# New orders for TensorE, ScalarE, VectorE and the one DMA queue in a convolution and attention kernel

## The reference

```python
# layer 0: 32 models of 16 channels; perception = x and its 8 shifts by one pixel, 144 channels a model
hdn = relu(einsum('bmchw,mdc->bmdhw', per_g, w1) + b1)          # 64 hidden channels a model
x = x + einsum('bmdhw,mcd->bmchw', hdn, w2) + b2
# layer 1: attention over the 1024 pixels, 128 inner channels
theta = einsum('oc,bcn->bno', theta_w, xf) + theta_b
phi = einsum('oc,bcn->bon', phi_w, xf) + phi_b[:, None]
g = einsum('oc,bcn->bno', g_w, xf) + g_b
attn = softmax(einsum('bno,bom->bnm', theta, phi), axis=-1)
z = einsum('co,bno->bcn', w_w, einsum('bnm,bmo->bno', attn, g)) + w_b
z = (z - bn_mean) * bn_gamma / sqrt(bn_var + 1e-5) + bn_beta
out = z + x
```

## Time and profile before

| | |
|---|---|
| median of 3 runs | 1632.85 us (1629.54 to 1635.52) |
| the profiled execution | 1621.29 us, of it the span of the profile 1619.5 us |
| TensorE matmuls | busy 1521.1 us, 94% of the span |
| VectorE, ScalarE, GpSimd | busy 867.7, 764.3 and 266.2 us |
| transfers | 361.84 MB, mean 223 GB/s |

### The profile page before, as it was taken

How to read it: one execution, slowest core, us unless ns; L and a number is a source line. 1 busy time by engine, 2 the same in 40 slices (tenths; PEclk the granted TensorE clock), 3 DMA queues, 4 the chain that set the end, 5 groups by cost and what they waited for, 6 DMA issues and landing times.

```text
span 1619.5 us, 23832 instructions
## 1 busy us (share of the span) xinstructions
PE 1521.1 (94%) x8324; PEld 846.5 (52%) x8324; DVE 867.7 (54%) x1200; ACT 764.3 (47%) x1205; POOL 266.2 (16%) x134
## 2 busy tenths in 40 slices
PE   5889989999998999999999999999999999999976
PEld 1265544655545455554655546455554655546455
DVE  0256363654636556383664646456383654637465
ACT  2444454544544455454544544455455544545542
POOL 0021030211203021030211203021030301204021
PEclk9999999999999999999999999999999999999998
DMA  9674875859667495875849658595875849677234
GB/s 290 163 266 160 253 261 159 295 168 284 231 187 257 165 322 191 256 255 160 295 160 288 236 170 284 170 308 190 259 258 164 296 157 294 220 214 271 96 119 167
DMA packets 179006, 361.84 MB, mean 223 GB/s; under 512 B 12336, under 2 KB 120880, under 8 KB 178992
## 3 DMA queue, kind: packets, MB, share of 16 engines
q1 hardware_dynamic: 178992, 361.66, 68.6%
HBM read 252.56 MB, written 109.05 MB: 223 GB/s over the span
## 4 chain that ended last, share of the span: by engine, by line
PE 78%; DMA 12%; DVE 4%; ACT 2%; issue 2%; SPq 1%; DVEq 0%; ACTq 0%
PE ps L413 24%; PE ps L433 8%; PE ps L424 7%; DMA x_lo<-rows_out 5%; PE ps L449 5%; PE ps L451 5%; PE ps L450 5%; DMA rows_out<-probs 4%; PE ps L479 4%; PE ps L481 4%; PE ps L480 4%; PE ps L493 2%; PE ps L464 2%; DVE probs L778 2%; PE ps L465 2%
## 5 line engine op out<-in xcount | busy, mean ns | idle before, releaser
L413 PE MATMUL ps<-windows,w_main 128*64 128x512 f32 x2048 | 488.2, 606 | 26.4 <-DMA windows<-in_x 13.2
L926 POOL TENSOR_TENSOR probs<-probs,row_inv 128x1024 f32<-128x1024 f32 x128 | 265.5, 2084 | 1326.2 <-DVE row_inv L766 1326.2
L611 ACT ACTIVATE hidden<-ps,columns 128x512 f32<-128x512 f32 x512 | 314.9, 688 | 309.5 <-PE ps L424 176.4
L413 PEld LDWEIGHTS ps<-windows,w_main 128*64 128x64 f32 x2048 | 129.4, 136 | 318.0 <-issue 203.0
L634 ACT ACTIVATE probs<-ps,neg_max 128x1024 f32<-128x1024 f32 x128 | 142.7, 1115 | 186.6 <-DVE neg_max L760 164.2
L741 DVE SCALAR_TENSOR_TENSOR x<-ps,columns,windows 128x512 f32<-128x512 f32 x128 | 95.9, 749 | 226.0 <-PE ps L433 195.5
L760 DVE TENSOR_REDUCE neg_max<-ps 128x1 f32<-128x1024 f32 x128 | 154.6, 1208 | 58.3 <-PE ps L466 56.1
L433 PE MATMUL ps<-hidden,w2s 128*32 128x512 f32 x1024 | 143.6, 634 | 32.3 <-ACT hidden L611 32.3
L787 DVE TENSOR_TENSOR x_lo<-x_lo,x_hi 128x1024 fp32r<-128x1024 f32 x128 | 165.2, 1301 | 15.3 <-ACT x_hi L641 15.2
L479 PE MATMUL ps<-x_hi,arena 128*128 128x256 f32 x512 | 152.6, 298 | 21.9 <-DVE arena L793 12.7
L778 DVE STREAM_TRANSPOSE probs<-probs 128x1024 f32<-128x1024 f32 x128 | 156.3, 1231 | 18.4 <-POOL probs L926 10.1
(11 more groups left out here) (55 smaller groups left out, 1520.8 us busy)
## 6 DMA issues: line engine op xcount, KB each, us to landing
windows<-in_x SPq DMA_DIRECT2D x208, 562.0 KB, 12.8
rows_out<-probs SPq DMA_DIRECT2D x128, 512.0 KB, 3.9
x_lo<-rows_out SPq DMA_DIRECT2D x128, 512.0 KB, 4.2
out<-x SPq DMA_DIRECT2D x64, 512.0 KB, 3.4
windows<-in_x SPq DMA_DIRECT2D x32, 421.5 KB, 9.6
windows<-in_x SPq DMA_DIRECT2D x32, 409.9 KB, 11.0
windows<-in_x SPq DMA_DIRECT2D x32, 281.0 KB, 7.1
rows_out<-hidden SPq DMA_DIRECT2D x16, 512.0 KB, 5.1
```

Source lines behind the costliest of these rows:

```text
L413: mm(ps[rows, hidden_bank(s, q), :], w_main[:, p, which, :], shifted(windows[:, w, :], unit // UNITS, half), start=True, stop=False, skip_ ...
L611: activation(hidden[:, q, :], ps[:, hidden_bank(s, q), :], ACT.Relu, bias=b1s[:, column:column + 1]).then_inc(hidden_ready, 1)
L926: nc.gpsimd.tensor_tensor(rows, rows, row_inv[:, e].to_broadcast([P, PIXELS]), ALU.mult).then_inc(normalized, 1)
```

## The change

No instruction is added or taken away, and no wait is changed; four lists are put in a new order. On SyncE `send_row(n, 0)` moves ahead of the second window call, the rows, g and their fetches are put in another sequence, and `store_quarter(n, 2)` moves behind `store_quarter(n, 3)`. On TensorE the first two scores move ahead of `project(n, 0, G)`, `scores(n, 2)` ahead of `project(n, 1, TH)`, `dx(n + 1, 0)` ahead of `main(n + 1, 1, 0)`, and several steps of layer 0 change places with steps of the attention. On ScalarE and VectorE the steps follow.

```diff
@@ -310,31 +310,32 @@
             def batch(n, has_next, has_second):
                 if has_next:
                     load_freed(n + 1, 3, 0)
+                send_row(n, 0)
+                if has_next:
                     load_freed(n + 1, 3, 1)
-                send_row(n, 0)
+                fetch_row(n, 0)
                 send_row(n, 1)
-                fetch_row(n, 0)
                 send_g(n)
+                send_row(n, 2)
                 fetch_row(n, 1)
-                send_row(n, 2)
                 fetch_g(n)
+                fetch_row(n, 2)
                 send_row(n, 3)
-                fetch_row(n, 2)
                 fetch_row(n, 3)
                 send_row(n, 4)
+                send_row(n, 5)
                 fetch_row(n, 4)
-                send_row(n, 5)
+                fetch_row(n, 5)
                 store_quarter(n, 0)
-                fetch_row(n, 5)
+                send_row(n, 6)
                 store_quarter(n, 1)
-                send_row(n, 6)
                 send_row(n, 7)
                 fetch_row(n, 6)
                 fetch_row(n, 7)
-                store_quarter(n, 2)
                 if has_second:
                     load_freed(n + 2, 0, 0)
                 store_quarter(n, 3)
+                store_quarter(n, 2)
                 if has_second:
                     load_freed(n + 2, 1, 0)
                     load_freed(n + 2, 1, 1)
@@ -517,11 +518,11 @@
                 dx(n, 7)
                 project(n, 0, PH)
                 project(n, 1, PH)
-                project(n, 0, G)
                 scores(n, 0)
                 scores(n, 1)
+                project(n, 0, G)
+                scores(n, 2)
                 project(n, 1, TH)
-                scores(n, 2)
                 scores(n, 3)
                 project(n, 1, G)
                 scores(n, 4)
@@ -530,35 +531,35 @@
                     hidden_shared(n + 1, 0)
                 scores(n, 5)
                 if has_next:
+                    dx(n + 1, 0)
                     mains(n + 1, 1, range(0, 1))
-                    dx(n + 1, 0)
                 scores(n, 6)
                 attend(n, 0, has_next)
+                scores(n, 7)
+                output(n, 0, 0)
                 if has_next:
                     mains(n + 1, 1, range(1, 3))
-                output(n, 0, 0)
-                scores(n, 7)
                 output(n, 0, 1)
...
                 if has_next:
-                    hidden_shared(n + 1, 1)
                     mains(n + 1, 2, range(0, 4))
                     mains(n + 1, 3, range(0, 1))
                     hidden_shared(n + 1, 2)
+                attend(n, 2, has_next)
+                if has_next:
                     dx(n + 1, 1)
-                attend(n, 2, has_next)
-                if has_next:
-                    dx(n + 1, 2)
+                output(n, 2, 0)
+                if has_next:
                     mains(n + 1, 3, range(1, 4))
                     hidden_shared(n + 1, 3)
-                output(n, 2, 0)
+                    dx(n + 1, 2)
+                    mains(n + 1, 4, range(0, 4))
                 output(n, 2, 1)
...
@@ -567,11 +568,11 @@
                 output(n, 3, 1)
                 if has_next:
                     mains(n + 1, 5, range(0, 4))
+                    hidden_shared(n + 1, 5)
                     dx(n + 1, 4)
-                    hidden_shared(n + 1, 5)
                     mains(n + 1, 6, range(0, 4))
+                    dx(n + 1, 5)
                     hidden_shared(n + 1, 6)
-                    dx(n + 1, 5)
                     mains(n + 1, 7, range(0, 4))
                     hidden_shared(n + 1, 7)
                     dx(n + 1, 6)
@@ -659,20 +660,18 @@
                 bias_projection(n, 0, TH)
                 bias_projection(n, 0, PH)
                 bias_projection(n, 1, PH)
+                exp_rows(n, 0)
                 bias_projection(n, 0, G)
-                exp_rows(n, 0)
                 exp_rows(n, 1)
                 bias_projection(n, 1, TH)
                 exp_rows(n, 2)
+                exp_rows(n, 3)
                 bias_projection(n, 1, G)
-                exp_rows(n, 3)
+                round_row(n, 0)
                 exp_rows(n, 4)
-                round_row(n, 0)
-                if has_next:
-                    relus(n + 1, 0, range(0, 2))
+                if has_next:
+                    relus(n + 1, 0, range(0, 4))
                 round_row(n, 1)
-                if has_next:
-                    relus(n + 1, 0, range(2, 4))
                 round_g(n)
                 exp_rows(n, 5)
                 round_row(n, 2)
...
                 round_row(n, 5)
+                round_y(n, 2)
                 if has_next:
                     relus(n + 1, 2, range(0, 4))
-                    round_x1(n + 1, 0)
-                    round_x1(n + 1, 1)
-                round_y(n, 2)
                 round_row(n, 6)
                 round_row(n, 7)
                 if has_next:
-                    round_x1(n + 1, 2)
...
@@ -819,19 +814,19 @@
                 find_max(n, 0)
                 find_max(n, 1)
                 invert_sum(n, 0)
+                transpose_row(n, 0)
                 invert_sum(n, 1)
+                find_max(n, 2)
                 split_projection(n, 1, TH)
-                transpose_row(n, 0)
-                find_max(n, 2)
+                invert_sum(n, 2)
+                find_max(n, 3)
                 transpose_row(n, 1)
-                find_max(n, 3)
-                invert_sum(n, 2)
-                transpose_g(n)
+                transpose_row(n, 2)
                 find_max(n, 4)
                 invert_sum(n, 3)
-                transpose_row(n, 2)
+                transpose_g(n)
+                transpose_row(n, 3)
                 invert_sum(n, 4)
-                transpose_row(n, 3)
                 split_row(n, 0)
...
@@ -839,49 +834,47 @@
                 find_max(n, 6)
                 invert_sum(n, 5)
                 split_row(n, 2)
+                invert_sum(n, 6)
                 transpose_row(n, 4)
                 split_y(n, 0)
-                invert_sum(n, 6)
+                transpose_row(n, 5)
+                add_out(n, 0, 0)
                 split_row(n, 3)
-                add_out(n, 0, 0)
                 find_max(n, 7)
-                transpose_row(n, 5)
                 add_out(n, 0, 1)
+                invert_sum(n, 7)
+                transpose_row(n, 6)
                 split_y(n, 1)
-                invert_sum(n, 7)
+                transpose_row(n, 7)
                 add_out(n, 1, 0)
...
```

More of the change, by code:

```diff
@@ L544, in batch @@
                     mains(n + 1, 1, range(3, 4))
+                    hidden_shared(n + 1, 1)
                 output(n, 1, 0)
@@ L683, in batch @@
                 round_y(n, 1)
+                if has_next:
+                    relus(n + 1, 1, range(0, 2))
                 round_row(n, 4)
                 if has_next:
-                    relus(n + 1, 1, range(0, 4))
+                    relus(n + 1, 1, range(2, 4))
                 round_row(n, 5)
+                round_y(n, 2)
                 if has_next:
                     relus(n + 1, 2, range(0, 4))
-                    round_x1(n + 1, 0)
-                    round_x1(n + 1, 1)
-                round_y(n, 2)
                 round_row(n, 6)
@@ L699, in batch @@
                 if has_next:
-                    relus(n + 1, 4, range(0, 2))
-                    round_x1(n + 1, 3)
-                    relus(n + 1, 4, range(2, 3))
-                if has_next:
-                    relus(n + 1, 4, range(3, 4))
-                    relus(n + 1, 5, range(0, 3))
-                if has_next:
-                    relus(n + 1, 5, range(3, 4))
-                if has_next:
-                    relus(n + 1, 6, range(0, 3))
+                    round_x1(n + 1, 0)
+                    relus(n + 1, 4, range(0, 3))
+                    round_x1(n + 1, 1)
+                    round_x1(n + 1, 2)
+                    relus(n + 1, 4, range(3, 4))
+                    relus(n + 1, 5, range(0, 4))
+                    relus(n + 1, 6, range(0, 3))
+                    round_x1(n + 1, 3)
+                    relus(n + 1, 6, range(3, 4))
                     round_x1(n + 1, 4)
                     round_x1(n + 1, 5)
-                    relus(n + 1, 6, range(3, 4))
-                if has_next:
                     relus(n + 1, 7, range(0, 4))
@@ L878, in batch @@
                 if has_next:
+                    sum_x1(n + 1, 3)
+                    sum_x1(n + 1, 4)
+                    split_x1(n + 1, 0)
+                    sum_x1(n + 1, 5)
+                    split_x1(n + 1, 1)
+                    split_x1(n + 1, 2)
                     split_x1(n + 1, 3)
-                    sum_x1(n + 1, 4)
-                    sum_x1(n + 1, 5)
                     split_x1(n + 1, 4)
+                    sum_x1(n + 1, 6)
                     split_x1(n + 1, 5)
-                    sum_x1(n + 1, 6)
```

19 lines of the change are left out of this document (5 added, 14 removed).

## The result

The changed kernel takes 1679.76 us, median of 4 runs (1678.04 to 1685.88), against 1633.62 us for the kernel before beside it (4 runs, 1629.54 to 1635.52): a ratio of 1.0306 with an interval of 1.0272 to 1.034. The forecast was 1650 with a range up to 1668. The direction was right, the size was not: +46 us instead of +17.

What follows compares the result with a forecast made beforehand. Bound: the first 38.82 us of a pass, where TensorE waits for relus and g behind the DMA queue. 15 x 1.0 + 2 = 17 on 1621.29 gives 1638.3; with the median 0.71% above, 1650 us, range 1626 to 1668.

Steps and rivals of the forecast that it cites:

- The 1.6 us ahead of the scores: TensorE, every pass: a new wait of some 1.6 us before scores(0), ended by VectorE's last lo part.
- rival (a): The wait ahead of the scores also brings the clock down: 1677 at worst, 1665 if in half the passes; chance 0.14.
- (b): Queue: four windows pass in 5.6 us, attend(0) starts at 806.1 as before, nothing changes: 1630 to 1636; chance 0.12.
- (c): Faster: (b), and short waits leave the clock at 1.00: 1623 to 1627, 1610 if falls vanish; chance 0.20.
- row 0 back at 797.6: Queue: row 0 lands at 788.7, then four windows 7.5 us and its fetch 1.35, back as before the change.
- 2.6: Queue: us for row 0 to reach DRAM when sent into an empty queue.
- I take 7.5: Queue: us the second call's four windows need, taken from 7.9 and 6.9 in two passes.
- The fetch of g took from 798.91 to 803.74: Queue: 4.8 us for g's fetch, so g is back at 805.0 and attend(0) starts at 807.4 against 806.10.
- the stretch of 58.37 can shrink by up to 0.6: TensorE from attend(0) on: shrinks by up to 0.6 us, so +1.0 us a pass, between 0.75 and 1.35.
- passes of about 98.2 us: Sign expected in the new profile: passes of this length, with a clock of 0.97.
- about 2.5 us: TensorE: the one wait ahead of dx(n+1,0), with one clock fall counted, 1.7 to 1.9 us.
- both chains, relus and g: Two ways to attend(0), through ScalarE's relus and TensorE (807.5) and through g (807.4): 1.3 to 1.4 us later.

Runs made afterwards that it cites:

- e3: Changed kernel with one edit undone: the second window call again ahead of send_row(n, 0); 1653.92 us, ratio 1.015.
- e1: Kernel before with one edit: send_row(n, 0) ahead of the second window call; 1703.36 us, ratio 1.0458.
- e10: Changed kernel, row 0 still sent first, with windows 3 and 18 loaded behind the fetch of row 3; 1647.54 us, ratio 1.0114.
- e6: Changed kernel with the second window call ahead of send_row(n, 0) again and windows 3 and 18 late behind fetch_row(n, 3); 1650.81 us, ratio 1.0077.
- e4: Kernel before with windows 3 and 18 taken out of the second window call and loaded behind fetch_row(n, 3); 1597.04 us, ratio 0.9799.
- e9: e6 with transpose_g moved back ahead of find_max(4) and main(n+1,1,0) back ahead of dx(n+1,0); 1623.25 us, ratio 0.9954.
- e7: Kernel before with scores(0) and scores(1) ahead of project(n, 0, G), and exp_rows(0) ahead of that projection's bias; 1646.52 us, ratio 1.0047.
- e8: Kernel before with dx(n+1,0) ahead of main(n+1,1,0) on TensorE; 1653.05 us, ratio 1.007.
- e12: e4 with transpose_row(0) ahead of invert_sum(1) and split_projection(1,TH) on VectorE; 1605.37 us, ratio 0.9865.
- e2: Changed kernel with SyncE's whole list of the kernel before; 1655.86 us, ratio 1.0149.
- e5: e3 with transpose_g moved ahead of find_max(4) on VectorE; 1641.7 us, ratio 1.0026.

## Why the prediction was wrong

*The places and most of the mechanisms were right.* The 1.6 us ahead of the scores came as 1.56 to 1.57 in every pass, with no fall of the clock, so rival (a) is out; row 0 left 1.5 us earlier in the pass (19.0 for 20.5) and lost it behind the windows; behind `attend(0)` nothing was lost (58.10 us); the last pass took +3.1 for a forecast of +2, within 0 to +3 but for 0.1. Rivals (b) and (c) needed four windows to pass in 5.6 us: they took 8.6.

*The step that failed is the size of three terms of one chain.* The prediction put row 0 back at 797.6, 30.3 us into the pass; it was back at 32.0. It went out 0.2 later than worked out and took 3.0 us for "2.6"; the windows took 8.6 for "I take 7.5". Next, `send_g` went at 29.06 into the pass, as worked out, but landed 1.5 later (34.5), since the fetch of row 0 ahead of it was late. Then came "The fetch of g took from 798.91 to 803.74", 4.8 us: it took 6.1. Over the passes it took 5.5 to 6.7 us, 6.0 on average, and in before 4.5 to 6.0, 5.2 on average, so the 4.8 of pass 7 was also a short one. Before, it was issued 4.4 us behind the fetch of row 1 and 2.7 ahead of that of row 2; now, behind the late row 0, all three were issued within 2.5 us. The rate of before's queue from 798 to 804, in which g came back, reads

```profile
GB/s 396 335 321 389 369 396 389 375 478 416 464 437 444 382 410 430 341 382 355 321 328 348 321 253 321 266 287 362 403 410 416 437 403 430 410 423 321 341 403 362
```

and is up to three times that of the row of after. What these two chains gave, 1.3 to 1.4 us a pass, was then cut to 1.0, since "the stretch of 58.37 can shrink by up to 0.6"; that part became 0.06 us shorter on average. `round_g` came at 40.6 for 37.7, `attend(0)` at 43.0 for 40.2. Over the loop it is 101.03 for the "passes of about 98.2 us", 2.8 a pass and 42 in all. In profiles the forecast was 1638.3 and the execution 1685.88, 47.6 more: these 42, 1 in the last pass and 4 ahead of the loop, where nothing was changed. In medians it is 30, since before's profile lay 12 us under its median and after's lay 6 above.

*The clock was named, but the wait ahead of it was sized too small.* The wait ahead of `dx`, "about 2.5 us", was 3.3 to 4.9, in the pass shown 4.08, longer by 1.6 as row 0 was later by 1.7, and the clock fell in all 15 passes; before, it fell in 12. In 9 of the 15 passes the fall is covered, since `attend(0)` then waits 0.5 to 0.9 us for g anyway, as the row at 837.32 shows; in 6 TensorE's own slow way ends last.

*What the experiments add.* The exchange on the queue makes about half of the loss (e3; e1 and e10 bear it out). The other half, 1.5%, is in the orders of the engines. With the queue short these orders cost 2.8% (e6 against e4): 1.2% for g two steps late with `dx` ahead of the pair (e6 against e9), and 1.6% for what e9 still has of the change (e9 against e4). There the rows name g, which leaves 2.4 us later than in e4, and waits behind `attend(0)`. The prediction had both chains, relus and g, and took them as equal; in e4, e6 and e9 g ends last in every pass, in after in 9 of 15. The early start of the scores costs 0.1 to 0.9 us a pass by the ratio of e7, not surely its 1.56, and in part through g. The kernel before lost time to the queue too: with two windows late (e4) it is 2.0% faster, and this, not the new order, is what its first 38.8 us asked for. The prediction had worked out that the four windows take "7.5" of the queue, and did not ask which of them could come later.

What stays open: no run takes g late and `dx` ahead of the pair apart with the queue short, and none puts the scores, or row 2's transpose, back in the kernel after, so the second half has no price for each order. In e8 no run takes the clock and the path apart: it holds the pair's 1.0 us that lay in a wait, and a longer fall. Nor does a run show why the set of windows took 8.6 us here and 7.9 and 6.9 in the earlier trace rows.

## What to carry to other kernels

Where one queue passes transfers in turn, a round trip (row out, row back) costs what stands between its landing and its fetch as much as what stands ahead of it; look for loads there that nobody reads soon and move those, checking what store they then hold. Price a transfer from rows in which the same neighbours share the queue, and from several passes, not from one in which it passes alone. Where two chains end at the same place, follow each back through every engine: here `transpose_g`, 2 us and more later on VectorE, came back as a later `attend(0)`. Work that stands between two waits fills one of them; before moving it behind the second, count the two as one wait, with the clock's fall.

## What the runs showed of the hardware

Fetches in packets of 1 KB that followed each other passed slowly: 102 to 314 GB/s from 829 to 833.5 in after; and packets of the same size passed at 253 to 478 in before from 798 to 804, where sent rows were among them. The Trainium skill, "DMA: Bandwidth & Descriptors", section "Specifications", puts the least transfer for the line rate at 512 B. With 1 KB the row of after stays under the rate of before, but in its slowest slices the DMA engines also stood idle for more than half of the time, so it isn't shown that the size of the packets is the reason.

The granted clock fell behind waits, and not only long ones. In e9, with one wait of 1.4 to 1.8 us a pass behind the scores' 1.56, and in e4, with two of 0.9 to 2.6 and 0.4 to 1.7, no wait of the loop brought it down; it was low only at the start of the first pass, from a fall ahead of the loop. In e12 it fell in 4 of 14 passes behind waits of 2.0 to 2.3 us, but not behind others of 2.0 to 2.2; in e10, with 0.91 and then 1.6 to 2.6 us, it fell in 10 of 15, the shortest a pair of 0.91 and 1.79. A longer wait can pass without a fall: one of 2.7 us with one of 1.6 behind it in e2, one of 3.04 with one of 1.8 in e5. Behind waits of 3.3 us and more (e8, after) it fell every time. What decides between 1.8 and 3.0 us these runs don't show. Falls are to the lower level, 1.2 GHz: the 5.2 us from `dx` on in after, of which a part is back at 2.4 GHz, show 0.67.

```profile
831.20:836.40 5.20, 5.19 (x18) 1.66 (x18) 1.69 (x3) 2.49 (x3) 0.72 (x1) 0.67 0.90 298
```
